# Corner sums of a deformable convolution: the sum of the two halves is moved from TensorE and VectorE to GpSimd

## The reference, cut to what is computed

```python
def deform_conv(x, off, w):           # N,C,H,W = 4,128,32,32; 9 taps; two layers of it
    py = rows + DY + off[:, :, 0];  px = cols + DX + off[:, :, 1]
    y0 = floor(py); x0 = floor(px); wy = py - y0; wx = px - x0
    ...
    cols = corner(y0i, x0i, (1-wy)*(1-wx)) + corner(y0i, x0i+1, (1-wy)*wx) \
         + corner(y0i+1, x0i, wy*(1-wx)) + corner(y0i+1, x0i+1, wy*wx)
    return einsum('nckhw,ock->nohw', cols, w.reshape(Co, C, K))
...
out = relu(batchnorm(deform_conv(x,   offsets(conv3x3(x)),   dcn1_w)))
out = relu(batchnorm(deform_conv(out, offsets(conv3x3(out)), dcn2_w)) + x)
# then per image: q, k, v = 1x1 convolutions; softmax(q^T k) over axis 1; v @ attn * gamma + input
```

## Time and profile before

| | us |
|---|---|
| measured, median of 3 runs | 781.89 |
| measured, lowest and highest | 781.34, 785.77 |
| profiled execution, span from first to last instruction | 930.4 |
| PE busy in it | 773.5 |
| DVE busy | 597.9 |
| ACT busy | 501.1 |
| POOL (GpSimd) busy | 483.8 |

### The profile page before, as it was taken

One profiled execution on the slowest core, in us unless ns is written; L12 is line 12 of the kernel. 1 busy time (PEld: TensorE's weight loads), 2 busy tenths in 40 slices (PEclk: granted clock), 3 DMA queues, 4 the chain that ended last, 5 costly groups with the idle time before them and its releaser, 6 DMA issues.

```text
span 930.4 us, 12479 instructions
## 1 busy us (share of the span) xinstructions
PE 773.5 (83%) x3497; PEld 469.0 (50%) x3497; DVE 597.9 (64%) x1605; ACT 501.1 (54%) x1269; POOL 483.8 (52%) x458
## 2 busy tenths in 40 slices
PE   7288798996879876973978979797887989989997
PEld 7245464553445443462536535353443544467887
DVE  4175579685657663952956868485665668876752
ACT  2174566665646563635655647474555555666432
POOL 3647557676667666325766657576667652000000
PEclk7579899997999988975989979898999889899999
DMA  6727646655565546336476555565555551000001
GB/s 213 253 80 226 193 137 179 182 149 148 150 190 158 148 139 189 92 111 206 142 225 180 156 152 150 151 171 157 159 170 172 160 156 57 1 1 1 24 24 46
DMA packets 55104, 130.14 MB, mean 140 GB/s; under 512 B 8271, under 2 KB 24944, under 8 KB 55036
## 3 DMA queue, kind: packets, MB, share of 16 engines
q0 software_dynamic: 35200, 115.37, 42.4%
q1 hardware_dynamic: 19820, 13.94, 4.8%
q10 hardware_dynamic: 16, 0.03, 0.0%
HBM read 118.76 MB, written 10.55 MB: 139 GB/s over the span
## 4 chain that ended last, share of the span: by engine, by line
PE 51%; another core or an unknown queue 17%; ACT 11%; DVE 10%; issue 9%; DMA 1%; DVEq 0%; ACTq 0%; SPq 0%
PE pair L1334 16%; PE pair L1347 6%; PE bank L1489 4%; ACT V L620 4%; ACT U L622 3%; PE bank L1285 3%; PE bank L1287 3%; PE pair L1320 3%; DVE V L926 2%; DVE U L926 2%; PE pair L1339 2%; PE pair L1449 2%; PE pair L1424 2%; DVE ST L976 2%
## 5 line engine op out<-in xcount | busy, mean ns | idle before, releaser
L538 POOL DMA_INDIRECT G<-table,rowi x440 | 475.9, 1082 | 292.3 <-DVE U L926 143.8
L1334 PE MATMUL pair<-ST,XT 128*128 128x512 f32 x544 | 270.6, 631 | 13.2 <-issue 9.6
L976 DVE TENSOR_TENSOR ST<-pair,stacks 128x512 f32<-128x512 f32 x180 | 119.7, 685 | 103.1 <-remote 83.6
L620 ACT ACTIVATE V<-G,wgt 128x128 f32<-128x128 f32 x440 | 175.0, 398 | 0.7 <-DMA G<-table,rowi 0.3
L622 ACT ACTIVATE U<-G,wgt 128x128 f32<-128x128 f32 x440 | 172.7, 393 | 0.0
L1334 PEld LDWEIGHTS pair<-ST,XT 128*128 128x128 f32 x544 | 109.8, 204 | 119.5 <-issue 96.8
L689 ACT COPY CT<-bank 128x512 f32<-128x512 f32 x110 | 64.3, 584 | 184.8 <-remote 116.2
L926 DVE SCALAR_TENSOR_TENSOR V<-G,wgt,V 128x128 f32<-128x128 f32 x440 | 152.4, 346 | 3.8 <-issue 3.8
L926 DVE SCALAR_TENSOR_TENSOR U<-G,wgt,U 128x128 f32<-128x128 f32 x440 | 152.7, 347 | 0.0
L1285 PE MATMUL bank<-band,V 128*128 128x128 f32 x440 | 105.6, 287 | 54.6 <-issue 31.7
L976 DVE TENSOR_TENSOR ST<-bank,stacks 128x512 f32<-128x512 f32 x92 | 63.0, 685 | 126.8 <-remote 97.1
(11 more groups left out here) (173 smaller groups left out, 769.3 us busy)
## 6 DMA issues: line engine op xcount, KB each, us to landing
table<-XT SPq DMA_DIRECT2D x16, 512.0 KB, 4.5
G<-table,rowi POOLq DMA_INDIRECT x440
out_dram<-G SPq DMA_DIRECT2D x8, 256.0 KB, 2.0
X<-in_x_dram SPq DMA_DIRECT2D x3, 512.0 KB, 6.5
A<-in_L_conv_dcn_w_dram SPq DMA_DIRECT2D x2, 576.0 KB
X<-in_x_dram SPq DMA_DIRECT2D x2, 256.0 KB, 2.9
table<-zeros SPq DMA_DIRECT2D x4, 16.0 KB, 2.1
qkv_nat<-in_L_conv_wv_dram SPq DMA_DIRECT2D x1, 64.0 KB
```

The costliest lines, as they stand in the source:

```text
L538: pool.indirect_dma_start(G[:, i % UNITS, r, :], None, table(n).rearrange("r (e k) -> r e k", e=2), bass.IndirectOffsetOnAxis(rowi[:, at:a ...
L620: act.activation(V[:, i % V_RING, r, :], G[:, i % UNITS, r, 0:C], ACT.Copy, scale=wgt[:, tile:tile + 1, 0])
L976: dve.tensor_tensor(ST[:, all_y % ST_RING, :], sel_acc[all_y % SEL_RING], HX[:, d % 2, :], ALU.mult).then_inc(st_ready[l], 1)
L1334: pe.matmul(dense_acc, XT[:, g // IGROUPS * TS + t, :], ST[:, all_y % ST_RING, :], start=(t == 0), stop=(t == QT - 1)).then_inc(dense_mm[l ...
```

## The change

GpSimd takes over `add_halves` for all blocks, `V = V + U` in one instruction of 128 x 512 float32. Before the gathers of block i (i >= 4) it waits for all four tiles of block i-4, adds its halves, and then issues the four gathers with no wait between them. The adds of the last four blocks of a layer follow its last gather. VectorE's adds are gone, and TensorE turns four tiles a block everywhere. It waits for GpSimd's add (`halves_added`) where it waited for `corner`.

```diff
-    ADD_STEPS = [()] * (GROUPS - 1) + [tuple(range(STEPS[GROUPS - 1]))]
...
+            def add_halves(l, i):
+                pool.wait_ge(corner[l], GTILES * (i + 1))
+                pool.tensor_tensor(V[:, i % V_RING], V[:, i % V_RING], U[:, i % V_RING], ALU.add) \
+                    .then_inc(halves_added[l], 1)
+
             for l in range(LAYERS):
                 pool.wait_ge(fill_out, 16 * FILLS)
                 for i, (g, s) in enumerate(BLOCKS):
...
+                    if i >= UNITS:
+                        add_halves(l, i - UNITS)
                     for r in range(GTILES):
-                        if i >= UNITS:
-                            pool.wait_ge(corner[l], GTILES * (i - UNITS) + r + 1)
-                            pool.nop(nofuse=True)
                         at = block_tile(i) + r
                         pool.indirect_dma_start(
...
+                for i in range(NB - UNITS, NB):
+                    add_halves(l, i)
...
-                def add_halves(i):
-                    if BLOCKS[i][1] in ADD_STEPS[BLOCKS[i][0]]:
-                        dve.wait_ge(corner[l], GTILES * (i + 1))
-                        dve.tensor_tensor(V[:, i % V_RING], V[:, i % V_RING], U[:, i % V_RING], ALU.add) \
-                            .then_inc(halves_added[l], 1)
...
-                add_halves(1)
...
-                    if more:
-                        add_halves(i + 2)
...
                 def turn(i):
-                    by_dve = BLOCKS[i][1] in ADD_STEPS[BLOCKS[i][0]]
-                    if by_dve:
-                        pe.wait_ge(halves_added[l], added(i + 1))
-                    else:
-                        pe.wait_ge(corner[l], GTILES * (i + 1))
+                    pe.wait_ge(halves_added[l], i + 1)
                     if i:
                         pe.wait_ge(turned_cp[l], i)
                     for r in range(GTILES):
-                        to = turn_bank[:, r * P:(r + 1) * P]
-                        last = pe.matmul(to, V[:, i % V_RING, r, :], ident, start=True, stop=by_dve, is_transpose=True)
-                        if not by_dve:
-                            last = pe.matmul(to, U[:, i % V_RING, r, :], ident, start=False, stop=True,
-                                             is_transpose=True)
+                        last = pe.transpose(turn_bank[:, r * P:(r + 1) * P], V[:, i % V_RING, r, :], ident)
                     last.then_inc(turned[l], 1)
```

More of the change, by code:

```diff
@@ L341, in casts_step @@
             return g + 2, {3: "top", 5: "middle"}.get(s + SOONER[g + 2])
-        def added(i):
-            return sum(s in ADD_STEPS[g] for g, s in BLOCKS[:i])
         def table(n):
```

## The result

| | before | after |
|---|---|---|
| measured, median | 781.7 us | 900.9 us |
| lowest and highest | 781.3, 785.8 | 899.1, 904.6 |
| profiled execution, span | 930.4 us | 897.3 us |

The ratio is 1.153, with a 95% interval of 1.149 to 1.157: 119 us slower, on a forecast of 133. The two profiled spans go the other way: 33 us less, where 0 to 55 more was expected. A reader who compared span with span would call the change 33 us faster.

A forecast was written before the change was run, and what follows sets the result against it. GpSimd's gathers were taken to bound both layers, with TensorE just behind. The measured 782 us plus 130 for adds in 100 blocks plus 3 at the layers' starts and ends gave 915 us, range 800 to 960.

The forecast's parts named there:

- GpSimd was a bound before the change: Both layers: without the profiler GpSimd's gathers set the pace, 5.0 us a block, with TensorE just behind.
- The stops of the earlier trace: Standstills with no named releaser, 17% of the 930.4 us span, about 155 us, said to belong hardly to measured executions.
- TensorE at 4.6 us a block: Blocks 5 to 54: TensorE as pacer would give about 40 us less than GpSimd as pacer.
- The add at 1.0 us: GpSimd's add of halves, once a block: 1.0 us plus a 0.30 us gap, 1.3 us a block (0.7 to 1.8).
- 100 blocks x 1.3 = 130: Blocks 5 to 54 of both layers: GpSimd's adds lengthen the time by 130 us.
- The 3 us for the layers' ends: Early adds delaying block 5 and the last add being on GpSimd: together 3 us.
- The sum of 770: Kernel before with GpSimd as pacer: two times 250 us for blocks 5 to 54, plus 270 of fixed parts.
- The new wait of TensorE: TensorE's turn waiting for an add in GpSimd's queue: adds latency, covered by the ring, and no period.
- Clock: TensorE idling 2 us in each 6.3 keeps its full clock, so no loss was counted.
- Rival A: The profiler also slows GpSimd, gather pitch 1.1 instead of 1.25 us: 845 us, range 785 to 860, chance 0.20.
- Rival B: SBUF contention between GpSimd's add and VectorE's corner sums: 950 us, or 1010 with 2.4 us adds; above 950, chance 0.10.
- Rival C: GpSimd has room and TensorE paces, so 42 us of matmuls come out: 740 us, range 740 to 785, chance 0.08.

The follow-up runs named there:

- the block wait alone: The change's order and its one wait per block for four tiles, without its adds; TensorE sums in all blocks: 783.6 us, ratio 1.012 to the kernel before.
- GpSimd lightened: The kernel before with three gathers a block instead of four from block 4 on: 768.3 us, ratio 0.987.
- both together: The kernel before with three gathers a block from block 4 on, and the matmuls of U and the add left out: 729.3 us, ratio 0.937.
- the first experiment: The kernel before with the matmuls of U left out and no add on any engine: 775.9 us, ratio 1.001.
- the free add: The block wait alone plus a same-shape GpSimd add into unused memory in 51 blocks a layer, for which nobody waits: 883.3 us, ratio 1.138 to the kernel before.
- the memsets: As the free add, but with two GpSimd memsets of 128x512 float32 in place of the add: 866.3 us, ratio 1.115 to the kernel before.
- VectorE's adds: The kernel before with VectorE adding the halves of every block, TensorE turning four tiles a block and GpSimd only gathering: 779.3 us, ratio 1.006.

## Why the prediction was right, and where not

1. **GpSimd was a bound before the change.** Shown, with TensorE level with it. Taking work from TensorE alone changed the time by 0.1%, and adding it to GpSimd cost in proportion. If the DMA engines and not POOL's queue had paced the gathers, the adds could have run in their shadow; the period grew by 1.1 us for 1.13 us of add. The busy shares of the earlier trace rows hid the bound. The three stretches of the earlier trace rows showed POOL at 5.4 us a block, and 5.34 is what it takes when it never waits. There is no undisturbed profile of the kernel before, so which of the two engines led in which part of it stays open.

2. **The stops of the earlier trace rows belonged to that profiled execution.** Borne out, though what made them stays unknown. In the ten other profiled executions the unknown share of the chain is absent, and the span agrees with the measured time: 897.3 and 900.9 after the change, 780.9 and 783.6 with the block wait alone. So it isn't a cost that the profiler always has. It was one disturbed execution. The forecast of the profiled span, 930 to 985, took it that such stops would come again, and failed with that.

3. **TensorE at 4.6 us a block, some 40 us below GpSimd.** This step was wrong. With GpSimd lightened TensorE's floor came out 9 us below, not 40. The two are nearly level. It is 5.0 to 5.2 us a block there. The 4.6 was read from 51 us of selected stretches, which hold less extra work than the average block: 4.7 matmuls of L1334 a block against 5.2 over blocks 5 to 54, and no offset product (L1196), of which blocks 5 to 54 of each layer hold 32. The earlier trace rows had already said so: PE was busy 296.04 us over 55 blocks, 5.4 a block, at a mean granted clock of 0.93. It didn't enter the sum, because past the change GpSimd is the slowest by far. It also means that the kernel before had no single bound: lightening TensorE is worth 0, lightening GpSimd 9, both together 48 us.

4. **The add at 1.0 us, 1.3 us a block with its gap.** The add took 1.27 us (median 1.273), above the value taken and inside the bounds of 0.61 and 1.46. The gap was the other way: not 0.30 more, but 0.14 less than between two gathers. Net 1.13 us. The two errors, 0.27 too little and 0.44 too much, cancel in part, and that is luck. The Trainium skill, "GPSIMD Engine Reference", section 3.1, speaks of about half VectorE's speed for two inputs; here it was 1.27 against 0.70 us, 1.8 times.

5. **100 blocks x 1.3 = 130.** The mis-sized term, and by item 4. In the block-wait profile blocks 5 to 54 took 5.30 us each in layer 0 (first gather's start 43.1 to last one's end 308.0) and 5.34 in layer 1 (358.9 to 625.8). After the change it was 6.43 and 6.39 (45.2 to 366.5, 422.2 to 741.6). The difference is 1.1 us, 110 in all. With the 9 us of the block wait's kernel over the kernel before that is 119, as measured. The 3 us for the layers' ends were about right: the last turn comes 11.9 and 12.1 us behind the last gather, against 9.4 and 10.4 with the block wait alone. The sum of 770 that stood for GpSimd as the pacer was near by luck. A block takes 5.34 us and not 5.0 in the first experiment's profile, which makes 34 us more. The fixed parts are 780.9 - 534.5 = 246 us there and not 270, since stops had hit them in the profile before: block 5 of layer 0 begins at 45.2 after the change, not at 54.8.

6. **The new wait of TensorE costs no period.** Shown within 12 us by the free add. In the blocks themselves POOL waited for corners only twice for longer than 0.5 us, 2.0 us each, which bounds it to 4 us there. The rest of what it costs is latency at the layers' ends.

7. **Clock.** I counted no loss, judging by an idle of 1.78 us. The granted clock over 310 to 340 us was 0.83. Of the two turns below, the first ran at a granted clock of 1.00 (304.9 to 307.0), the second, behind an idle of 2.98 us, at 0.50 (311.6 to 314.0), which is 1.2 GHz:

```profile
305.04 0.66 PE L1273 MATMUL bank<-band,V 128*128 128x128 f32 x4 [1.19 <-POOL V L522]
```
```profile
311.69 1.12 PE L1273 MATMUL bank<-band,V 128*128 128x128 f32 x4 [2.98 <-POOL V L522]
```

So the clock did fall at times, and the reading was too simple. It cost no time here, as GpSimd's adds go on at 6.64 and 6.25 us through both rows.

8. **Rival A** (the profiler slows POOL) falls: the pitch of 1.25 us stands in executions whose span equals the measured time. **Rival B** (contention) is right in its mechanism and mostly wrong in who pays. Its figure of 1010 us for an add of 2.4 us doesn't follow either: 1.4 us more in each of 100 blocks would be 1055. One corner sum that an add fell upon, with its neighbours before it:

```profile
302.80 0.34 DVE L928 SCALAR_TENSOR_TENSOR U<-G,wgt,U 128x128 f32<-128x128 f32 x1
303.06 0.34 DVE L928 SCALAR_TENSOR_TENSOR V<-G,wgt,V 128x128 f32<-128x128 f32 x1
303.33 1.82 DVE L928 SCALAR_TENSOR_TENSOR U<-G,wgt,U 128x128 f32<-128x128 f32 x1
```

The add ran from 303.72 to 304.99, and the corner sum that had begun at 303.33 ended at 305.15 instead of 303.67. The Trainium skill, "SBUF — State Buffer", states for the shared port pair that the loser blocks for the whole instruction and that a GpSimd operation takes part if it reads SBUF; both the 1.82 us and the memsets that left VectorE at 344 ns agree. Of the 880 corner sums 75 took over 0.6 us. Each of them overlaps an add and ends 0.16 us behind the add's end. In 67 the corner sum's row begins before the add's; the rows don't show whether it was already at work or stood waiting from its start. VectorE had room for all this. GpSimd paid where an add was held: 8 of the 110 adds took over 1.35 us, six of them 1.64 to 1.68 and the one at each layer's end 3.15. That is some 6 us in all (mean 1.329 against a median of 1.273), not the 35 of the rival. **Rival C** falls by the first experiment: its 42 us come out only when GpSimd is lightened too.

No version here beats the kernel before while computing the same. VectorE's adds come nearest, and are 0.6% behind.

## What to carry to other kernels

An engine that is busy for only half of the time can be the bound: look at its pitch with the gap in front of each instruction, and in stretches where the favourite is never idle count who advances more. Before moving work from one engine to another ask for the price on the receiver per round of the loop, and lighten each suspect alone and both together, since with two level bounds a single cut shows little or nothing. Compare the profile's span with the measured time before any row of it is used. And read an engine's time per round over the whole loop, as a few clean stretches can leave out work that comes only now and then: here they gave TensorE 4.6 us instead of 5.0 to 5.2.

## What was not expected of the hardware

The profiled execution of the kernel before held some 150 us of stops with no releaser, that none of the ten other profiles here shows. GpSimd's compute instructions start right behind a gather (309.41 + 0.94 = 310.35, add at 310.36), where the next gather leaves 0.30 us. And an add of GpSimd can stretch a VectorE instruction fivefold, 0.34 to 1.82 us, even one whose row begins before the add's. The other way round it happened once a layer: an add beside a row of corner sums took 3.15 us.
